# Constant products on TensorE during the first transfer, and the context's norms moved into the first cross attention

## The reference

```
x = x + tanh(g_xattn[0]) * _L0_xattn_ref(_layernorm(x), ctx, ctx, ...)   # 16 heads of 8
x = x + tanh(g_ffn[0])   * _L0_ffn_ref(_layernorm(x), ...)               # top 1 of 8 experts
x = x + tanh(g_xattn[1]) * _L1_xattn_ref(_layernorm(x), ctx, ctx, mask, ...)
x = x + tanh(g_ffn[1])   * _L1_ffn_ref(_layernorm(x), ...)               # top 2 of 8 experts
...
```

```
k = layer_norm(key_antecedent @ Wk, gk, bk)
v = layer_norm(value_antecedent @ Wv, gv, bv)
```

## Time and profile before

| | |
|---|---|
| runs, median (lowest to highest) | 1061.17 us (1059.9 to 1061.2), 3 runs |
| the profiled execution | 1049.98 us, of it the span 1047.8 us |
| mean granted TensorE clock in it | 0.932 |
| PE busy | 920.8 us (88%) |
| DVE busy | 778.0 us (74%) |
| ACT busy | 557.4 us (53%) |
| POOL busy | 495.5 us (47%) |

### The profile page before, as it was taken

How to read it: one execution, slowest core, us unless ns; L and a number is a source line. 1 busy time by engine, 2 the same in 40 slices (tenths; PEclk the granted TensorE clock), 3 DMA queues, 4 the chain that set the end, 5 groups by cost and what they waited for, 6 DMA issues and landing times.

```text
span 1047.8 us, 19571 instructions
## 1 busy us (share of the span) xinstructions
PE 920.8 (88%) x6337; PEld 658.4 (63%) x6337; DVE 778.0 (74%) x2080; ACT 557.4 (53%) x1494; POOL 495.5 (47%) x467
## 2 busy tenths in 40 slices
PE   6999895898778999779987698988989999989987
PEld 4787633777678999647774243434437677668873
DVE  5989998999767877779995576776734644589982
ACT  3775556896445555624442166666754233445533
POOL 5444554676066664535556667574530600024430
PEclk8999896999789999879999579999999999999998
DMA  9300000000111111500000322221002000000001
GB/s 327 150 1 1 2 6 1 1 1 1 42 39 44 40 47 32 168 1 1 0 1 30 106 59 79 60 85 47 24 18 84 1 1 1 1 2 2 1 1 40
DMA packets 29829, 40.56 MB, mean 39 GB/s; under 512 B 11468, under 2 KB 25036, under 8 KB 29228
## 3 DMA queue, kind: packets, MB, share of 16 engines
q1 hardware_dynamic: 27244, 34.28, 10.4%
q0 software_dynamic: 2496, 5.16, 1.9%
HBM read 31.44 MB, written 7.82 MB: 37 GB/s over the span
## 4 chain that ended last, share of the span: by engine, by line
PE 27%; issue 14%; POOL 8%; DVE 5%; ACT 2%; SPq 1%; DMA 0%; DVEq 0%; POOLq 0%; ACTq 0%
POOL att L1794 6%; PE ps L1169 4%; PE ps L835 4%; PE ps L825 4%; PE ps L1141 4%; PE ps L1153 3%; PE ps L799 1%; PE ps L1255 1%; PE ps L1263 1%; DVE rs L2141 1%; SPq L576 1%; PE ps L1107 1%; DVE stats L2017 0%; DVE U L2045 0%; PE ps L1112 0%
## 5 line engine op out<-in xcount | busy, mean ns | idle before, releaser
L1794 POOL TENSOR_TENSOR att<-att,ri 128x1232 f32<-128x1232 f32 x64 | 163.1, 2549 | 157.8 <-DVE ri L2147 157.8
L799 PE MATMUL ps<-VW,PT 128*128 128x128 f32 (+3 forms) x1280 | 157.6, 278 | 13.1 <-DVE x L2162 11.3
L799 PEld LDWEIGHTS ps<-VW,PT 128*128 128x128 f32 (+1 forms) x1280 | 148.4, 192 | 30.7 <-DVE x L2162 23.7
L1376 ACT ACTIVATE PT<-ps 128x512 f32<-128x512 f32 x128 | 70.5, 594 | 84.2 <-PE ps L772 83.5
L772 PE MATMUL ps<-W,att 128*128 128x128 f32 (+1 forms) x640 | 86.1, 281 | 15.1 <-POOL att L1794 13.6
L1768 POOL TENSOR_TENSOR rstd<-ve,minus_half 128x4 f32<-128x4 f32 x38 | 38.8, 1037 | 116.4 <-DVE ve L2032 99.8
L835 PEld LDWEIGHTS ps<-U,att 128*128 128x128 f32 x512 | 67.2, 194 | 33.7 <-issue 29.6
L2598 DVE CUSTOM_DVE_ANT_0 C<-ps,cmaskb 128x512 bf16<-128x512 f32 (+1 forms) x128 | 71.0, 554 | 19.6 <-PE ps L1141 16.8
L772 PEld LDWEIGHTS ps<-W,att 128*128 128x128 f32 (+1 forms) x640 | 72.0, 142 | 21.2 <-POOL att L1794 14.4
L2141 DVE TENSOR_REDUCE rs<-att 128x16 f32<-128x1232 f32 (+1 forms) x64 | 83.6, 1306 | 1.9 <-ACT att L1362 1.6
L2598 DVE CUSTOM_DVE_ANT_0 U<-ps,cmaskb 128x384 bf16<-128x384 f32 (+1 forms) x128 | 53.9, 421 | 41.6 <-PE ps L1141 41.3
(11 more groups left out here) (433 smaller groups left out, 2116.7 us busy)
## 6 DMA issues: line engine op xcount, KB each, us to landing
U<-in_ffn SPq DMA_DIRECT2D x1, 6176.0 KB, 23.0
U<-split SPq DMA_DIRECT2D x144, 32.0 KB
W<-split SPq DMA_DIRECT2D x144, 32.0 KB
W<-in_packed SPq DMA_DIRECT2D x1, 2162.5 KB, 23.9
U<-in_ffn SPq DMA_DIRECT2D x1, 2060.0 KB, 9.6
U<-in_moe SPq DMA_DIRECT2D x1, 2048.0 KB, 7.4
split<-VBD SPq DMA_DIRECT2D x4, 384.0 KB, 2.9
split<-W SPq DMA_DIRECT2D x4, 384.0 KB, 2.8
```

The lines of the kernel that those rows point to most:

```text
L799: q = mm(attended(s, t), PT[0:m, t.slot(2), c, :], batch(VW, t.group)[0:m, c * D:(c + 1) * D], start=(c == 0), stop=(c == NC - 1))
L1376: go(PT[:, t.slot(2), 4 * k:4 * k + 4, :].rearrange("p c n -> p (c n)"), ps[:, k0 + k, :], ACT.Copy).then_inc(probsT, 1)
L1794: tt(p, p, over_keys(ri[:, t.slot(2), :]), ALU.mult).then_inc(probs, 1)
```

## The change

Three things change.

1. TensorE waits for `consts` 1 (a small fill that GpSimd does first) and then issues 12 products of a constant, 128x128 in f32, into a bank of PSUM that is overwritten later, ahead of its wait for the first transfer.
2. The moments of the raw keys and values, the sum into `1wq` and both norms leave F0. They go to X0's loop on VectorE, at the end of its ticks 1 and 2 (moments) and 4 and 5 (norms), with scratch of their own (`c_stats`, `c_mv`, `c_ve`, `c_rstd` in `q1_s`) and semaphores of their own. The two roots on GpSimd become one (77x8) after its third multiplication. GpSimd's scale and shift of the values stay behind its roots of F0, and now wait only for norms made in X0.
3. VectorE's and GpSimd's loops over X0 are written out for all 16 tiles.

```diff
+LOADING = 12
...
             ident = w("ident")
+            pe.wait_ge(consts, 1)
+            half = minus_half[:, 0:1].to_broadcast([P, P])
+            for _ in range(LOADING):
+                mm(ps[:, 7, 0:P], half, half, start=True, stop=True)
             pe.wait_ge(ld["a"], 16)
...
-                pe.wait_ge(s_xn, TB * (ROUND0[X1] - KV1 + 1))
+                pe.wait_ge(context_xn, TB)
...
-                skewed_loop(pool, [(normalize, 0)], NT, TB)
+                def context_root(t):
+                    if t.n == 2:
+                        pool.wait_ge(context_chain, KV1 * (2 * TB + 1))
+                        tt(c_rstd[0:KEYS, :], c_ve[0:KEYS, :], minus_half[0:KEYS, 0:1].to_broadcast([KEYS, KV1 * TB]), ALU.pow)\
+                            .then_inc(consts, 1)
+                if s == X0:
+                    skewed_loop(pool, [(normalize, 0), (context_root, 0)], NT, NT)
+                else:
+                    skewed_loop(pool, [(normalize, 0)], NT, TB)
...
-            for r in range(KV1):
-                root(ROUND0[X1] - KV1 + r, r)
...
-            pool.wait_ge(s_xn, TB * ROUND0[X1])
+            pool.wait_ge(context_xn, KV1 * TB)
...
+            def context_moments(r):
+                at = slice(r * TB, (r + 1) * TB)
+                made = (2 * TB + 1) * r
+                dve.wait_ge(kv_sb, KV_SB0[X3])
+                for i in range(TB):
+                    v.bn_stats(c_stats[0:KEYS, r * TB + i, :], raw_row(r, i)).then_inc(context_chain, 1)
+                dve.wait_ge(context_chain, made + TB)
+                for i in range(TB):
+                    v.bn_aggr(c_mv[0:KEYS, r * TB + i, :], c_stats[0:KEYS, r * TB + i, :]).then_inc(context_chain, 1)
+                dve.wait_ge(context_chain, made + 2 * TB)
+                ts(c_ve[0:KEYS, at], c_mv[0:KEYS, at, 1], LN_EPS, None, ALU.add).then_inc(context_chain, 1)
+
+            def context_normed(r):
+                for i in range(TB):
+                    k = r * TB + i
+                    ts(kv_rows[r][:, i, :], raw_row(r, i), c_mv[0:KEYS, k, 0:1], c_rstd[0:KEYS, k:k + 1],
+                       ALU.subtract, ALU.mult).then_inc(context_xn, 1)
...
+                def context_rows(t):
+                    if s != X0:
+                        return
+                    if 1 <= t.n < 1 + KV1:
+                        context_moments(t.n - 1)
+                    elif 2 + KV1 <= t.n < 2 + 2 * KV1:
+                        dve.wait_ge(consts, 2)
+                        if t.n == 2 + KV1:
+                            tt(w("1wq"), means_s, w("1wq"), ALU.add).then_inc(consts, 1)
+                        context_normed(t.n - 2 - KV1)
...
-                skewed_loop(dve, steps + [(last_rope, 0), (update, 3), (early_moments, 3)], NT, TB)
+                skewed_loop(dve, steps + [(last_rope, 0), (update, 3), (early_moments, 3), (context_rows, 0)], NT, NT if s == X0 else TB)
...
-            for r in range(KV1):
-                moments(n0 - KV1 + r, kv[r], r, rows=KEYS)
-            tt(w("1wq"), means_s, w("1wq"), ALU.add).then_inc(consts, 1)
...
-            normed_context(0)
             gate(F0, 0, 0, tg[:, 4:5])
-            normed_context(1)
```

More of the change, by code:

```diff
@@ L65, in before @@
     return sum(B * table[i] for i in range(s)) + (kv if s > X1 else 0)
-ROUND0 = {s: before(ROUNDS, s, KV1) + (KV1 if s == X1 else 0) for s in range(9)}
+ROUND0 = {s: before(ROUNDS, s, 0) for s in range(9)}
 TURN0 = {s: before(TURNED, s, 1) + (1 if s == X1 else 0) + (B - 1 if s == X0 else 0) for s in range(9)}
@@ L280, in build @@
         means_s = q1_s[:, 0:D]
+        c_stats = q1_s[:, D:D + KV1 * TB * 6].rearrange("p (i k) -> p i k", k=6)
+        c_mv = q1_s[:, D + KV1 * TB * 6:D + KV1 * TB * 8].rearrange("p (i k) -> p i k", k=2)
+        c_ve, c_rstd = (q1_s[:, D + KV1 * TB * k:D + KV1 * TB * (k + 1)] for k in (8, 9))
         xT_at = (xnT_s[:, :], q1_s[:, :])
@@ L380, in build @@
         kv_ps, kv_sb, kv_chain = sem("kv_ps"), sem("kv_sb"), sem("kv_chain")
+        context_chain, context_xn = sem("context_chain"), sem("context_xn")
         pool_shifted = sem("pool_shifted")
@@ L1011, in turn_context @@
                 t.then_inc(turned, 1)
-            pe.wait_ge(consts, 2)
+            pe.wait_ge(consts, 3)
             for t in range(NT):
@@ L2046, in normed, with raw_row @@
                             .then_inc(s_xn, rounds)
+            def raw_row(r, i):
+                return raw_rows[:, (KV1 * i + r) * D:(KV1 * i + r + 1) * D]
+            def context_moments(r):
[14 more added lines that the diff above has]
+                       ALU.subtract, ALU.mult).then_inc(context_xn, 1)
             def xn_of(nth):
@@ L2476, in _ @@
             n0, t0 = ROUND0[X1], TURN0[X1]
-            dve.wait_ge(kv_sb, KV_SB0[X3])
-            kv = [lambda i, r=r: raw_rows[:, (KV1 * i + r) * D:(KV1 * i + r + 1) * D] for r in range(KV1)]
-            for r in range(KV1):
-                moments(n0 - KV1 + r, kv[r], r, rows=KEYS)
-            tt(w("1wq"), means_s, w("1wq"), ALU.add).then_inc(consts, 1)
-            def normed_context(r):
-                normed(n0 - KV1 + r, None, kv[r], lambda i: kv_rows[r][:, i, :], r, rows=KEYS)
-            normed_context(0)
             gate(F0, 0, 0, tg[:, 4:5])
-            normed_context(1)
             def add_experts(t):
```

## The result

The changed kernel took 1062.93 us (median of 20 runs, 1059.9 to 1068.9). The kernel before, timed beside it, took 1059.14 (20 runs, 1053.49 to 1063.22). The ratio is 1.0042, 95% interval 1.0028 to 1.0056: slower by 0.42%. Forecast were 4.2 us more; the medians differ by 3.8. The forecast's 1065.4 stands 2.5 us above the time; 2.0 of that come from its base, 1061.17, a median of only three runs of before.

A forecast was written before the change was run, and what follows sets the result against it. TensorE and VectorE, both nearly full and tied, bound the first cross attention. 4.9 us lost there less 0.7 back in the feed-forward stage gives 4.2, on 1061.17: 1065.4 us, range 1059.6 to 1069.0.

The forecast's parts named there:

- Constants: Kernel start: 12 products end at 6.3 us and speed TensorE's early passes; 1.9 us saved at most, 0.3 lost at worst.
- the cap by the tables: First cross attention: GpSimd's mask and bias tables last until 27.67, so its first multiplication comes at most 1.9 us earlier.
- My rival on the clock: TensorE's clock falls back before or in the first tiles; 6.5 or 8.3 us slower in total, chance 0.17.
- Tick 1: First cross attention: moments' last step held until GpSimd's tables end; tile 2's maxima at about 27.8, 1.8 us ahead.
- Tick 2: First cross attention: moments' last step held until GpSimd's multiplication ends at 34.65; tile 3's maxima only 0.1 us ahead.
- Ticks 4 and 5: First cross attention: sum and norms held by GpSimd's multiplication; tile 5 2.7 us late, tile 6 5.5, about 4.9 staying.
- The feed-forward stage: Behind the first cross attention: removing the context's work there gives 0.7 us back net.
- The spread keys: Feed-forward stage: four spread tables on VectorE no longer meet GpSimd's two operations on the values; 1.2 us off.
- the pair beside the norms: Feed-forward stage: GpSimd's two operations on the values alternate with VectorE's last norms of `x`; 0.6 us late.
- Loops: First cross attention: loops of VectorE and GpSimd written out save next to nothing, taken as 0.
- Rival 1: First cross attention: VectorE isn't held by GpSimd's multiplication; 1.0 to 2.0 us gained there, 1059.0 us total, chance 0.20.
- Rival 2: First tiles: TensorE's clock falls back before or in them; 1067.7 us, or 1069.5 with no front gain; chance 0.17.

The follow-up runs named there:

- the filling: 10 more constant products where TensorE waits for GpSimd's first multiplication, added to the kernel before with only the 12 constant products; ratio 0.9991 to before.
- the context behind the subtraction: The changed kernel with the context's VectorE instructions put behind the subtraction of the same tick instead of at its end; ratio 1.0007 to before.
- The run with the pair moved: Context's work behind the subtraction, plus GpSimd's scale and shift of the values put behind its multiplications of tiles 7 and 8; ratio 1.0000 to before.
- the context alone: The changed kernel without the 12 constant products: context's work moved and loops written out; ratio 1.0064 to before.

## Why the prediction was right, and where it wasn't

The sign, the size and the place were right, and so was the mechanism of the norms' ticks; several of the terms were not, and that their errors cancelled is luck.

- **Constants.** Their end (6.3 forecast, 5.93) and the cap by the tables (27.7, 27.52) held. That 1.9 us remain of it failed: alone they leave 0.0. The first products gave back more than the 2 us put down (tile 0's maxima 2.94 earlier), which the cap made worthless. My rival on the clock looked for the fall ahead of the first scores; it came behind them, in a wait that the cap itself makes, and the filling brought back 2.5.
- **Tick 1.** "Held until the tables end" failed: the step went in front of the second bias table, 0.25 long, and tile 2's maxima stood at 26.51 instead of 27.8. With the context behind the subtraction it was held for 1.04, again until the one operation that ran had ended. How long it is held depends on the moment at which it arrives.
- **Tick 2.** Held, as forecast (1.19), but 1.3 us earlier than I put it (the multiplication at 31.11, forecast 32.4): tile 3's maxima at 33.63, forecast 34.75. The 1.2 us by which they were still ahead were then lost on TensorE, whose scores for tile 4 were 1.91 us late.
- **Ticks 4 and 5.** Right to the size: tile 5's maxima at 48.06 (forecast 48.0), tile 6's at 55.69 (56.0), tile 15 at +4.48 (+4.9). This is by two errors that cancel. In front of the norms I had the kernel 0.1 ahead of before, and at tile 4 it was 0.46 behind, by TensorE's low clock; from there to tile 15 I had 5.0 us, and it was 4.0. Of the sum into `1wq` I had said that it would be held; it took its 0.28, GpSimd's multiplication grew by 0.15, and the first norm was held instead.
- **The feed-forward stage.** 0.7 us were to come back, 0.1 did. The spread keys are 1.5 shorter (1.2 forecast). The term that was too small is the pair beside the norms, 0.6: the norms are 2.0 longer, ScalarE's copy of the last batch comes 1.3 later (124.00 against 118.23, less the 4.5 brought along) and the gate 2.2 later (127.21 against 120.54). The run with the pair moved gives its price at layer 1, 1.0 us (1.89 come back from tile 15 to layer 1 instead of 0.86). What I had not counted is in the trace: TensorE's clock was at 0.50 from about 121 to 131, some 10 us, where it was there for 7 before. With the context behind the subtraction it was 7 again. That this length is the cause wasn't tried, and the other runs don't settle it: with the feed-forward stage as before, some 10 us of low clock stand beside 0.1 us lost (loops written out) and 0.6 (constants filled).
- **Loops.** Nothing, as forecast.
- **Rival 1** (not held) is refuted by the lengths, 1.19, 3.04 and 3.08, and by the run that moved the same instructions. Its price was added up wrongly: 1.9 less 0.7 and 0.6 leave 0.6 us, not 1.0 to 2.0, so 1059.9 and not 1059.0. **Rival 2** (the clock) was the mechanism of the front, though the total stayed the forecast's.

## What to carry to other kernels

A gain at the front is kept only if the next engine downstream isn't made to wait: here a 2 us earlier start ended in a 3 us wait for GpSimd, and TensorE's low clock took all of it. Before work is moved into a "free" half microsecond of VectorE, look at what GpSimd does at that very point of the tick; behind the subtraction the same nine instructions of ticks 4 and 5 cost 0.9 to 2.0 us instead of 4.0 at the end of the tick. And a premise about the clock that rests on one profiled execution should be looked for in a second one.

## What the runs showed of the hardware

- Where VectorE's `tensor_scalar` from SBUF to SBUF meets a long GpSimd operation, it waits for its end (3.04 for 1.10) and not for the operation behind it (0.25 in front of the second bias table). A sum of two SBUF inputs that started within 0.02 us of the multiplication took its usual 0.28 and the multiplication 2.40 for 2.25, in all three kernels that have this order. The row reductions and the statistics run beside it at their usual length.
- TensorE's clock doesn't fall at the same point in each execution of the same instructions. The 18 passes of the first fold took 4.05 us in before, 3.11 with the context alone, 2.66 with the loops written out, 2.17 and 4.05 in the two executions of one kernel. Between the last two tile 15 moved by 3.8 us. The Trainium skill (TensorE: Matmul & The Clock Gate, section What's actually happening) states it for the start of a kernel, with the same kernel measured at 6, 11 or 14 slow matmuls; the trace agrees there: the product L992 near 14.8 us took 1.12 us in before and 2.08, still half rate, with the loops written out. For the fall between 14 and 20 us the runs alone speak.
- In the first 13 us the granted clock reads 1.00 though the passes run at half rate: L699's eight took 3.69 us, and 1.95 behind the constants. With the loops written out it reads 1.00 up to 30 us, though the first scores (8 passes, 1.41 us for 0.80) ran at half rate at 17.89. Read the passes there, not the column.
- GpSimd's root on 77x8 took 1.66 us, on 128x4 1.03: two roots in one saved GpSimd 0.4 us.
